# Keys' transfers spread, rows normalised within the last attention batch, and the blocks' experts found behind the selection matrices

## What is computed

```python
x = x + L0_attn(layernorm(x))           # 16 heads of 16, causal, rope
x = x + L0_xattn(layernorm(x), ctx)     # gelu(x ctx^T) * (x ctx^T) ctx: a gated product with the context
x = x + L0_ffn(layernorm(x))            # mixture: 8 experts of 512, top 2, and a shared one
x = x + L1_attn(layernorm(x))           # 16 heads, not causal
x = x + L1_xattn(layernorm(x), ctx)     # cross attention; softmax over the QUERIES (axis=2)
x = x + L1_ffn(layernorm(x))            # mixture: 8 experts of 1024, top 2 with masked softmaxes
```

## Time and profile before

| | |
|---|---|
| runs of the kernel | median 1621.8 us (1618.25 to 1626.14, 3 runs) |
| the profiled execution | 1623.72 us, of which the span from first to last instruction is 1621.9 |
| TensorE | busy 1440.5 us, 89% |
| VectorE | 1178.2 us, 73% |
| ScalarE | 899.5 us, 55% |
| GpSimd | 627.7 us, 39% |
| mean granted TensorE clock | 0.94 |

### The profile page before, as it was taken

How to read it: one execution, slowest core, us unless ns; L and a number is a source line. 1 busy time by engine, 2 the same in 40 slices (tenths; PEclk the granted TensorE clock), 3 DMA queues, 4 the chain that set the end, 5 groups by cost and what they waited for, 6 DMA issues and landing times. The chain is left out here.

```text
span 1621.9 us, 30209 instructions
## 1 busy us (share of the span) xinstructions
PE 1440.5 (89%) x9918; PEld 995.4 (61%) x9918; DVE 1178.2 (73%) x2499; ACT 899.5 (55%) x1704; POOL 627.7 (39%) x917
## 2 busy tenths in 40 slices
PE   7899998989899999689999988988756899999996
PEld 3455454569899998333434332333244899999996
DVE  4767662554778888478878758888858688888884
ACT  1455553223256666046666687878812576767673
POOL 6445430010235655546445546457113232333221
PEclk8899998998999999779999998999987999999998
DMA  6223320120259886533223323223034677887872
GB/s 167 61 47 58 60 41 27 54 102 21 105 166 254 254 238 172 134 81 60 52 46 68 60 53 80 50 57 76 1 105 131 210 236 238 240 237 234 250 231 43
DMA packets 104553, 194.59 MB, mean 120 GB/s; under 512 B 30448, under 2 KB 55920, under 8 KB 101456
## 3 DMA queue, kind: packets, MB, share of 16 engines
q1 hardware_dynamic: 70864, 153.31, 30.1%
q0 software_dynamic: 33024, 38.97, 13.8%
q10 hardware_dynamic: 512, 0.40, 0.1%
HBM read 135.89 MB, written 18.61 MB: 95 GB/s over the span
## 5 line engine op out<-in xcount | busy, mean ns | idle before, releaser
L814 ACT ACTIVATE l1a_sb_probs<-l1a_s_ps,l1a_sb_kmax 128x512 f32<-128x512 f32 x256 | 172.5, 707 | 26.7 <-DVE l1a_sb_kmax L747 25.9
L747 DVE TENSOR_REDUCE l1a_sb_kmax<-l1a_s_ps 128x1 f32<-128x512 f32 x256 | 160.7, 677 | 34.1 <-PE l1a_s_ps L937 33.2
L712 DVE TENSOR_REDUCE l1a_sb_mx<-l1a_s_ps 128x2 f32<-128x1024 f32 x128 | 153.3, 1218 | 38.5 <-PE l1a_s_ps L898 38.4
L820 ACT ACTIVATE l1a_sb_probs<-l1a_s_ps 128x1024 f32<-128x1024 f32 x128 | 130.1, 1024 | 80.0 <-PE l1a_s_ps L937 79.7
L586 POOL DMA_DIRECT2D l1a_sb_kst<-l1a_sb_hi x252 | 124.7, 499 | 101.4 <-PE l1a_s_ps L937 96.3
L937 PEld LDWEIGHTS l1a_s_ps<-l1a_sb_qst,l1a_sb_kst 49*128 49x128 f32 (+1 forms) x512 | 48.7, 189 | 168.6 <-issue 96.7
L707 DVE CUSTOM_DVE_ANT_0 l0a_sb_seen<-l0a_s_ps,l0a_sb_above 128x128 f32<-128x128 f32 (+3 forms) x256 | 113.5, 487 | 52.2 <-PE l0a_s_ps L898 51.8
L2026 PE MATMUL l1m_g_ps<-l1m_sb_rows_hi,l1m_sb_hi 128*128 128x256 f32 x512 | 146.8, 287 | 0.0
L2026 PE MATMUL l1m_g_ps<-l1m_sb_rows_lo,l1m_sb_hi 128*128 128x256 f32 x512 | 145.3, 284 | 0.0
L2026 PE MATMUL l1m_g_ps<-l1m_sb_rows_hi,l1m_sb_lo 128*128 128x256 f32 x512 | 145.3, 284 | 0.0
L937 PE MATMUL l1a_s_ps<-l1a_sb_qst,l1a_sb_kst 49*128 49x512 f32 (+1 forms) x512 | 126.3, 503 | 18.5 <-ACT l1a_sb_probs L814 16.5
(11 more groups left out here) (407 smaller groups left out, 3941.4 us busy)
## 6 DMA issues: line engine op xcount, KB each, us to landing
l1m_sb_raw<-in_l1m_w SPq DMA_DIRECT2D x92, 512.0 KB
l0m_sb_raw<-in_l0m_w SPq DMA_DIRECT2D x72, 512.0 KB
l1m_sb_raw<-in_l1m_w SPq DMA_DIRECT2D x23, 1024.0 KB
l1a_sb_qst<-l1a_sb_hi SPq DMA_DIRECT2D x256, 32.0 KB, 2.2
l1a_sb_kst<-l1a_sb_hi POOLq DMA_DIRECT2D x252, 32.0 KB, 2.0
l0a_sb_qst<-l0a_sb_hi SPq DMA_DIRECT2D x128, 32.0 KB, 2.3
l1a_sb_qst<-l1a_sb_lo SPq DMA_DIRECT2D x128, 32.0 KB, 2.2
l1a_sb_kst<-l1a_sb_lo POOLq DMA_DIRECT2D x126, 32.0 KB, 2.1
```

Source lines behind the costliest of these rows:

```text
L712: dve.tensor_reduce(mx[:, g, qt, 2 * p:2 * p + 2], buffer("A", b, g, j)[:, :, :], AX.X, ALU.max).then_inc(a_max.sem, 1)
L747: dve.tensor_reduce(kmax[:, n % 4, e:e + 1], buffer("S", b, g, j)[:, e, :], AX.X, ALU.max, negate=True).then_inc(kmax_done.sem, 1)
L814: ins = act.activation(probs[:, n % 8, e, :], at[:, e, :], ACT.Exp, bias=kmax[:, n % 4, e:e + 1], accum_out=zsum[:, n % 4, e:e + 1])
L820: act.activation(probs[:, n % 8, :, c0:T], at[:, :, c0:T], ACT.Exp, scale=SCALE).then_inc(exp_done.sem, 1)
```

## The change

Four edits. (1) In cross attention, the keys of the next batch's group 0 are transferred by SyncE (three transfers a head, as before), right after the queries of that group; those of group 1 stay with GpSimd at slots 19 to 22; those of groups 2 and 3 are transferred by GpSimd within the batch itself, in eight of the slots 4 to 13. This holds for batches 5 to 7; the first cross batch (4) keeps its place. (2) In slots 2, 10 and 18 of the last batch, the rows of batches 0, 1 and 2 for the mixture's layer norm are made: statistics on VectorE, power and scaling on GpSimd, into raw13, which now is allocated before the attention. The mixture only normalises batch 3. Its first 12 idle matmuls become 6, and the others ahead of the logits are gone. (3) The second half of EXPERTS is a step of its own, BLOCKS, and in layer 1's mixture it stands, with LOAD, behind the selection matrices. In layer 0's it stays where it was. (4) The place in the tile in `held` is made by ScalarE, in both mixtures.

```diff
@@ def cross_slot @@
         if at == 19 and nxt is not None:
             yield "STACK", nxt, 0, 0
+            yield from keys(nxt, 0)
             yield "STACK", nxt, 1, 0
...
-        if at < GH:
-            yield "KEYS", b, NG - 1, at
-        if at >= 19 and nxt is not None and at < 19 + 3 * GH:
-            yield "KEYS", nxt, *divmod(at - 19, GH)
+        if nxt is None and at in (2, 10, 18):
+            yield "AHEAD", at // 8, 0, 0
+        if turned:
+            if at < GH:
+                yield "KEYS", b, NG - 1, at
+        elif b > 0 and kinds[b - 1] == "cross" and at in (4, 6, 8, 9, 10, 11, 12, 13):
+            yield "KEYS", b, *((2, (4, 6, 8, 9).index(at)) if at < 10 else (3, at - 10))
+        if nxt is not None and 19 <= at < 19 + GH:
+            yield "KEYS", nxt, 1, at - 19
@@ attention, SyncE (GpSimd's stack returns where by_sp holds) @@
+        def by_sp(b, g):
+            return g == 0 and b > 0 and kinds[b - 1] == "cross"
...
+            def keys_stack(b, g, head):
+                if not by_sp(b, g):
+                    return
+                p, e = 2 * g + head // 2, head % 2
+                hi_done.wait(sp, b, 1)
+                lo_done.wait(sp, b, 1)
+                s_ready.wait(sp, b - 1, 8 * g + 7)
+                for n, source in enumerate((hi, hi, lo)):
+                    sp.dma_start(in_stack(kst, p, e, n), in_part(source, 1, p, e)).then_inc(kfirst_sp[p], 16)
@@ attention, GpSimd @@
+            def norm_ahead(i, *_):
...
+                stats_ahead.wait(pool, i, 2 * NT - 1)
+                pool.tensor_tensor(rstd_a[:, i, 0, :], mv_a[:, i, :, 1], const["eps"][:, :], ALU.add
+                                   ).then_inc(rstd_ahead.sem, 1)
+                rstd_ahead.wait(pool, i, 0)
+                pool.tensor_tensor(rstd_a[:, i, 1, :], rstd_a[:, i, 0, :], const["minus_half"][:, :], ALU.pow
+                                   ).then_inc(rstd_ahead.sem, 1)
+                rstd_ahead.wait(pool, i, 1)
+                for t in range(NT):
+                    pool.tensor_scalar(normed[:, i, t, :], x[:, i * NT + t, :], mv_a[:, i, t, 0:1],
+                                       rstd_a[:, i, 1, t:t + 1], ALU.subtract, ALU.mult).then_inc(normed_ahead.sem, 1)
@@ attention, VectorE @@
+            def stats_of(i, *_):
...
+                x_added.wait(dve, B + i, 1)
+                for t in range(NT):
+                    dve.bn_stats(stats_a[:, i, t, :], x[:, i * NT + t, :]).then_inc(stats_ahead.sem, 1)
+                stats_ahead.wait(dve, i, NT - 1)
+                dve.memset(nothing[:, :], 0.0)
+                for t in range(NT):
+                    dve.bn_aggr(mv_a[:, i, t, :], stats_a[:, i, t, :]).then_inc(stats_ahead.sem, 1)
@@ moe_schedule @@
-    yield "IDLE", 20 if shared else 12, 0
+    yield "IDLE", 20 if shared else 6, 0
...
     else:
-        yield "IDLE", 7, 0
+        for b in range(AHEAD, B):
+            yield "LN1", b, 0
+            yield "LN2", b, 0
+        yield "TURN", 0, 0
         yield "TURN", 1, 0
         yield "LOGITS", 0, 0
-        yield "IDLE", 4, 0
-        yield "LN1", 3, 0
-        yield "LN2", 2, 0
         yield "TURN", 2, 0
         yield "LOGITS", 1, 0
-        yield "IDLE", 4, 0
-        yield "LN2", 3, 0
+        yield "LOGITS", 2, 0
         yield "TURN", 3, 0
-        yield "LOGITS", 2, 0
-        yield "IDLE", 4, 0
         yield "LOGITS", 3, 0
-        for step in ("TOP1", "TOP2", "RANK", "EXPERTS", "LOAD", "ROWS", "PLACES", "HELD"):
+        for step in ("TOP1", "TOP2", "RANK", "EXPERTS", "ROWS", "PLACES", "HELD"):
             yield step, 0, 0
         for c in range(NSPOT):
             yield "SPOT", c, 0
             yield "LIST", c, 1
+        yield "BLOCKS", 0, 0
+        yield "LOAD", 0, 0
@@ moe, GpSimd @@
                 for k in range(TOP):
-                    for n, part in enumerate((tile_first, in_tile)):
-                        pool.tensor_tensor(held[:, k, :, n, :], own[:, k, :, :], part, ALU.mult).then_inc(tokens_held, 1)
+                    pool.tensor_tensor(held[:, k, :, 0, :], own[:, k, :, :], tile_first, ALU.mult).then_inc(tokens_held, 1)
@@ moe, ScalarE @@
+            def held_in_tile(*_):
+
+                act.wait_ge(placed, 1)
+                for k in range(TOP):
+                    act.activation(held[:, k, :, 1, :], own[:, k, :, :], ACT.Copy, scale=const["token"][:, 0:1]
+                                   ).then_inc(in_tile_held, 1)
@@ route: experts is cut in two @@
+    def blocks(*_):
+        end = full("end")
         for k in range(2):
             then(dve.tensor_tensor(at["ends"][:, k, :, :], end[:, k, :].unsqueeze(1).to_broadcast([P, NBLK, E]),
```

More of the change, by code:

```diff
@@ L87, in wait, with __init__ @@
             eng.wait_ge(self.sem, value)
+class Tally:
+    def __init__(self, sem, per=1):
+        self.sem, self.per = sem, per
+    def wait(self, eng, n, step=0):
+        value = n * self.per + step + 1
+        if value > 0:
+            eng.wait_ge(self.sem, value)
 CHUNK = (0, 2, 1, 3)
+AHEAD = 3
 def keep_warm(pe, at, const, n):
@@ L408, in attention @@
         x_biased = steps("x_biased", 1)
+        stats_ahead, rstd_ahead, normed_ahead = (Tally(sem(n), per) for n, per in (
+            ("stats_ahead", 2 * NT), ("rstd_ahead", 2), ("normed_ahead", NT)))
         kmax_done = steps("kmax_done", 0, 2 * 8 * NG)
@@ L541, in _ @@
                              ).then_inc(ones_in, 16)
-            run({"STACK": stack, "LN1": before_batch, "CTX": context, "M": rows})
+            run({"STACK": stack, "KEYS": keys_stack, "LN1": before_batch, "CTX": context, "M": rows})
         @block.gpsimd
@@ L1254, in halves_to @@
     return sum(halves(n) for n in range(e % 2, e + 1, 2))
-class Tally:
-    def __init__(self, sem, per=1):
-        self.sem, self.per = sem, per
-    def wait(self, eng, n, step=0):
-        value = n * self.per + step + 1
-        if value > 0:
-            eng.wait_ge(self.sem, value)
 ALL, TOKENS, WEIGHTS = slice(0, 5), slice(0, 2), slice(2, 5)
@@ L1594, in moe, with normed @@
         block = ctx.enter_context(nc.Block())
+        def normed(eng, b):
+            if b >= ahead:
+                xn_done.wait(eng, b - ahead, NT - 1)
         def two_chunks(t, k, f):
@@ L2251, in row_weights @@
         then(dve.tensor_tensor(full("row_weight"), full("row_weight"), at["row_holds"][:, :, 4, :], ALU.add))
-    return {"TOP1": top1, "TOP2": top2, "UNMASKED": unmasked, "EXPERTS": experts, "SHARES": shares, "ROWS": rows,
+    return {"TOP1": top1, "TOP2": top2, "UNMASKED": unmasked, "EXPERTS": experts, "BLOCKS": blocks, "SHARES": shares, "ROWS": rows,
             "PLACES": places, "SPOT": spot, "LISTS": lists,
@@ L2273, in build @@
         moe(nc, "l0m", x, const, of("l0m"), 512, phi=False, shared=True)
-        attention(nc, "l1a", x, const, [("full", of("l1a")), ("cross", of("l1x") | context)])
-        moe(nc, "l1m", x, const, of("l1m"), 1024, phi=True, shared=False, out=out)
+        raw13 = ctx.enter_context(nc.sbuf_tensor("l1m_sb_raw13", [P, 1, 4, 2, CC, 2 * P], F32))
+        normed = raw13[:, 0, :, :, :, :].rearrange("p f n c d -> p f (n c) d")
+        attention(nc, "l1a", x, const, [("full", of("l1a")), ("cross", of("l1x") | context)], normed)
+        moe(nc, "l1m", x, const, of("l1m"), 1024, phi=True, shared=False, out=out, raw13=raw13)
 def rope_factor():
```

71 lines of the change are left out of this document (42 added, 29 removed).

## The result

The changed kernel takes 1625.8 us (median of 20 runs, 1617.6 to 1635.8), the kernel before 1620.8 us beside it (20 runs, 1614.4 to 1630.9): ratio 1.0032, interval 1.0018 to 1.0046. It is a little slower, inside the 0.5% that counts as no change, where 1612.8 and 9 us less were forecast. The profiled execution took 1629.6 us (span 1627.8) against 1623.7 (1621.9).

What follows compares the result with a forecast made beforehand. In cross attention VectorE was taken as fullest, about even with ScalarE, with gaps at batch turns; afterwards the mixture's head is one chain. -8.6 + 4 + 1 - 5.3 - 1.1 + 1 = -9.0 us, predicted 1612.8 us, eight-in-ten range 1600 to 1621.

Steps and rivals of the forecast that it cites:

- Part 1, the keys: Cross attention's batch turns: moving key transfers off GpSimd's queue there removes three large VectorE gaps, -8.6 us (-17 to 0).
- rival (a): Batch turns: they lose more than their gaps, all 17 us go and normalising is hidden, about 1599 us; chance 0.19.
- Rival (e): Slots 4 to 13: as full as the turn was, so the gaps move there, 1621.4 us; chance 0.06.
- Part 2, GpSimd: Last attention batch: normalising puts GpSimd's queue behind by up to 5 us against 4 of reserve, +1 us (0 to +15).
- Rival (d): Last batch: GpSimd's 128x256 scalings take 2 us each and stall the queue, slower than before, 1628 us; chance 0.05.
- The price of 0.75: Last batch: one 128x256 GpSimd scaling taken as half of the 128x512 row's 1.51 us, making a block 4.3 us.
- Part 2, VectorE: Last batch, slots 2, 10 and 18: statistics on VectorE delay the next maxima, +4 us (0 to 5.4).
- Part 3, the head: Layer 1's mixture up to routing: fewer warm-ups and three batches already normalised start routing earlier, -5.3 us (-6 to +4).
- Rival (c): Mixture's head gains nothing: low clock through most logits, or the gather waits for weights, about 1620 us; chance 0.06.
- Part 4: Layer 1's mixture: products moved to ScalarE shorten selection matrices by 1.1 us; later weights cost +1; moving blocks' experts costs 0.
- the prediction's estimate of twice its time: Mixture's gather beside the weight loads: at most twice its 4.5 us, taken as 0 (0 to +4) in the sum.

Runs made afterwards that it cites:

- experiment 4: The changed kernel with GpSimd's normalising cut into fifteen pieces, one a slot from slot 14 of the last batch: 1608.4 us, ratio 0.9928 to the kernel before.
- experiment 10: The kernel before with the keys' spreading, plus three statistics groups on VectorE in the last batch, none of GpSimd's normalising: 1615.0 us, ratio 0.9969 to the kernel before.

## Why the prediction was wrong, step by step

**Part 1, the keys (-8.6, bounds -17 to 0): right in mechanism and place, somewhat small.** In the changed kernel the turns lose 3.2, 4.5 and 1.4 us, 9.1 together; TensorE has no wait for scaled values there, and VectorE's waits for scores from 1003 to 1070 us are 4.9 us in all, none over 1.3. The third turn brings 1.4 and not the 2.87 taken for it, the first two bring more. By themselves the keys bring 15 us (9 to 20): 10.8 at the turns, 3 at the boundary, the rest cannot be told apart. Without the boundary, which stood in no forecast, that is 12, between the forecast's 8.6 and rival (a)'s 17. One reading behind the forecast was loose: at the second turn TensorE's wait of 3.22 us ended at 1066.16, 7.2 us ahead of the end of VectorE's gap; a second wait for scaled values, of 2.48 us and over at 1070.68, stands nearer. Rival (e) is out: slots 4 to 13 carried the heads.

**Part 2, GpSimd (+1, bounds 0 to 15): the step that failed.** It said "In front of the value scaling of that time there are about three slots, 4 us, before TensorE needs it." The three scalings in question had 1.23, 1.46 and 1.46 us. Three slots lie between scaling and product in the order of work, but the scaling has to wait for the inverse sums, and by then most of that time is gone; the next scores stand behind the product. So a block of 6.2 us is not weighed against the room in twelve slots but against the reserve of the one scaling behind it: 6.2 less 1.2 to 1.5 is 4.7 to 5.0 us a block. Measured were 13.6 us for three over the same work in pieces (69.4 against 55.7, experiment 4), 4.5 each. The rows that would have told the reserve were in the trace of before. Rival (d) had this mechanism and its sign, but a threshold of 1.5 us an instruction that rests on the same 4 us; it came about at 1.23. The price of 0.75 was off as well (half of the 128x512 row was taken; it is 81% of it), and so a block was 6.2 us and not 4.3.

By the Trainium skill ("GPSIMD Engine Reference", Engine selection) GpSimd is roughly at line rate with one input. The trace does not bear that out for this form: 1.23 us for 128x256 with two columns of scalars, where VectorE takes 1.38 us for four of them.

**Part 2, VectorE (+4, bounds 0 to 5.4): about 8.** The parity of the engines was seen, what the clock adds to it was not (4 of the 9.4 us of experiment 10). The upper bound was drawn from VectorE's own time and so was no bound.

**Part 3, the head (-5.3, bounds -6 to +4): +0.7, the second step that failed.** Rival (c), its low clock. The forecast read the warm-ups between the logits as filler against VectorE's rows. They also kept the clock at 1.00 for 15 us; turns and logits alone did not (0.50 from 1200.6 on). That this was possible stood in the bounds, with "may rise later"; it rose in time, and fell again.

**Part 4 (-1.1 and +1): right in each term.** Matrices -1.1, the weights' lateness +1.4 to +1.7, blocks' experts moved at no cost (-1.9 and +1.9), layer 0's mixture nothing. Not all of the +1.4 is VectorE's chain: TensorE turns the gathered rows 6.3 us behind the gather's issue (6.0 before) and takes 1.11 us for it (0.66 before), and VectorE takes its half of the split 0.7 us behind ScalarE's, where before it followed at once. The gather beside the four loads is thus 0.3 us later, and not the 4.5 that the prediction's estimate of twice its time allowed. As a whole the part was worth nothing, and its first half alone would have been worth 1.1.

**Not in the sum: the boundary, -3.1.** GpSimd's drain starts at its last scaling and ended 3.1 us behind all others. With 36 transfers fewer it ends before them.

The sum redone with the changed kernel's own numbers, from the start of the cross attention: -8.1 at and between the turns, +20.3 in the last batch, -3.1, +0.7, -1.1, +1.4 and -0.9 in the rest, 9.2 us, less the 3.4 us in which this execution happened to be ahead: 5.8. The medians say 5.0. The three parts run alone add up to about +1 us (-15, +16, 0); the 4 us between that and the 5.0 measured are less than the three intervals leave open, so whether the parts act on each other is not shown.

## What to carry to other kernels

Before work is put on an idle engine, look for the short instruction on it that others wait for, and measure the time from that instruction's end to its first reader; what a block takes beyond that time is paid each time (here 6.2 us against 1.2 to 1.5), and the same work in single pieces no longer than it can cost nothing. Look the pair up by number, and not by what stands closest on the timeline. Warm-ups that look like filler can be what holds TensorE's clock, so take the clock of the stretch into the price of taking them out. When a change has several parts, run each alone: here one was worth 15 us and another cost 16, and the sum showed neither.

## What the runs showed of the hardware that was not expected

GpSimd's drain at the end of a section: 10.5 us behind 186 transfers, 9.7 to 10.1 behind some 76 indirect ones, 9.22, 8.24 and 3.83 behind 378, 366 and 342 (the last in ten profiles), 0.98 behind none. It doesn't hang on how long ago the last transfer was: 9.22 us came 41 to 56 us after it, 3.83 came 25 to 46 us after it. An explicit drain in GpSimd's idle time takes its share away from the last one (10.1 to 5.9 us). What sets the length stays open: 12 transfers fewer took off 1.0 us and the next 24 took off 4.4, but with a single transfer since the explicit drain the last one still took 5.9 us, more than behind 342.

Statistics of 4.9 us on VectorE, where it is level with ScalarE, made the batch longer by nearly twice their length (9.4 us). TensorE's granted clock was 0.79 in that stretch and 0.93 without them. All three kernels with them have 0.76 to 0.79 there, five of six profiles without them 0.92 to 0.96, and the sixth has 0.80 and is 4.1 us longer than another profile of the same kernel. So about 4 us go with the clock and 5 with VectorE; that the statistics pull the clock down rests on this count of profiles alone.
